# One adding DMA per unit for the sum of the rotated keys, in an attention and feed-forward kernel

## The reference, cut to what matters

```python
def linear_attention(x, Wq, bq, Wk, bk, Wv, bv, g, bb):
    q = gelu(x @ Wq + bq) + 0.21
    k = gelu(x @ Wk + bk) + 0.21
    v = x @ Wv + bv
    q_r, k_r = rope(q), rope(k)          # rope(t) = t * cos + swapped_pairs(t) * sin
    ...                                  # split into 16 heads
    z = 1.0 / (einsum('bhnd,bhmd->bhnm', q, kmean) + 1e-06)
    kv = einsum('bhnd,bhne->bhde', k_r, v) / n
    out = einsum('bhnd,bhde->bhne', q_r, kv) * z
    return layernorm(out + x, g, bb)
```

## Time and profile before

| what | value |
|---|---|
| median of 3 runs | 1835.23 us (1830.85 to 1835.43) |
| the profiled execution | 1831.92 us |
| its span, first to last instruction | 1830.1 us |
| PE busy | 1807.1 us, 99% |
| PEld busy | 1477.9 us, 81% |
| DVE busy | 1454.8 us, 79% |
| POOL busy | 1016.3 us, 56% (over nine tenths within attention) |
| ACT busy | 937.0 us, 51% |
| share of PE in the chain that ended last | 96% |

### The profile page before, as it was taken

How to read it: one execution, slowest core, us unless ns; L and a number is a source line. 1 busy time by engine, 2 the same in 40 slices (tenths; PEclk the granted TensorE clock), 3 DMA queues, 4 the chain that set the end, 5 groups by cost and what they waited for, 6 DMA issues and landing times.

```text
span 1830.1 us, 46210 instructions
## 1 busy us (share of the span) xinstructions
PE 1807.1 (99%) x19196; PEld 1477.9 (81%) x19196; DVE 1454.8 (79%) x3454; ACT 937.0 (51%) x1741; POOL 1016.3 (56%) x775
## 2 busy tenths in 40 slices
PE   9999999999999999999999999999999999999998
PEld 3336888888888888888887988888888888888887
DVE  3667788888788888888887767888888888888887
ACT  5554776677667766677667742232323232323231
POOL 1557999999899999999984012222222222222221
PEclk9999999999999999999999999999999999999999
DMA  8372210100102210000105931010101010101000
GB/s 296 149 270 109 94 60 3 37 2 2 37 2 106 94 37 3 30 9 3 60 2 192 306 105 35 28 42 24 47 24 47 24 47 24 46 25 43 27 12 24
DMA packets 25234, 115.38 MB, mean 63 GB/s; under 512 B 4480, under 2 KB 5440, under 8 KB 19904
## 3 DMA queue, kind: packets, MB, share of 16 engines
q1 hardware_dynamic: 21104, 89.69, 13.9%
q0 software_dynamic: 1152, 12.58, 1.9%
q10 hardware_dynamic: 2768, 10.15, 1.5%
HBM read 80.95 MB, written 31.46 MB: 61 GB/s over the span
## 4 chain that ended last, share of the span: by engine, by line
PE 96%; DVE 2%; issue 1%; DMA 1%; ACT 1%; POOL 0%; ACTq 0%; SPq 0%; DVEq 0%; POOLq 0%
PE bankC L1449 13%; PE bankC L33 7%; PE bankC L32 7%; PE bankC L34 7%; PE ring L32 6%; PE ring L34 6%; PE ring L33 6%; PE bankC L1448 6%; PE big L934 5%; PE big L34 3%; PE big L33 3%; PE big L32 3%; PE ring L866 3%; PE big L846 3%; PE conv_ps L256 3%; PE hid_ps L245 3%
## 5 line engine op out<-in xcount | busy, mean ns | idle before, releaser
L1449 PE MATMUL bankC<-down,act_hi 128*128 128x512 f32 x992 | 353.1, 397 | 0.0
L1448 PE MATMUL bankC<-down,act_lo 128*128 128x256 f32 x868 | 246.2, 284 | 0.0
L1449 PEld LDWEIGHTS bankC<-down,act_hi 128*128 128x128 f32 x992 | 186.3, 188 | 41.9
L1574 DVE TENSOR_TENSOR act_lo<-gel,act_hi 128x512 fp32r<-128x512 f32 x256 | 210.6, 823 | 8.7
L33 PE MATMUL bankC<-aT_lo,up_hi 128*128 128x512 f32 x512 | 199.6, 390 | 0.0
L32 PE MATMUL bankC<-aT_hi,up_hi 128*128 128x512 f32 x512 | 199.5, 390 | 0.0
L34 PE MATMUL bankC<-aT_hi,up_lo 128*128 128x512 f32 x512 | 199.4, 389 | 0.0
L1528 POOL TENSOR_TENSOR hC<-hC,vecC 128x1024 f32<-128x1024 f32 x16 | 38.7, 2416 | 283.5 <-PE turn L1423 283.5
L1534 POOL TENSOR_TENSOR rstdC<-var_epsC,minus_halfC 128x4 f32<-128x4 f32 x47 | 56.1, 1193 | 249.2 <-DVE var_epsC L1602 249.2
L1448 PEld LDWEIGHTS bankC<-down,act_lo 128*128 128x128 f32 x868 | 164.1, 189 | 1.4
L774 POOL TENSOR_TENSOR kr<-kr,kc 128x512 f32<-128x512 f32 x128 | 161.8, 1299 | 0.0
(11 more groups left out here) (215 smaller groups left out, 5261.4 us busy)
## 6 DMA issues: line engine op xcount, KB each, us to landing
raw_late<-in_AB SPq DMA_DIRECT2D x30, 320.0 KB, 3.9
u<-hA SPq DMA_DIRECT2D x8, 1024.0 KB, 5.0
u_next<-u SPq DMA_DIRECT2D x8, 1024.0 KB, 5.9
hC<-u SPq DMA_DIRECT2D x16, 512.0 KB, 3.9
xC<-in_x SPq DMA_DIRECT2D x16, 512.0 KB, 4.8
out<-w_flat SPq DMA_DIRECT2D x15, 512.0 KB, 2.6
w_flat<-in_AB SPq DMA_DIRECT2D x22, 320.0 KB, 3.7
w_split<-w_parts ACTq DMA_DIRECT2D x4, 1536.0 KB, 5.8
```

The lines of the kernel that those rows point to most:

```text
L1448: e.matmul(bank[:, 0:H], a_lo[:, fb, tok], both[k][:, 0, fb, :], start=False, stop=False)
L1449: m = e.matmul(bank[:, :], a_hi[:, fb, tok], both[k][:, :, fb, :], start=fb == 0, stop=fb == FB - 1)
L1574: e.tensor_tensor(a_lo[:, fb, :], g, a_hi[:, fb, :].bitcast(F32), ALU.subtract).then_inc(s_act_lo, 1)
```

## The change

`sum_k` loses its index u. GpSimd waits until all four parts of the unit are rotated, and then issues one DMA with an adding accumulate, which reads `kc` and adds it to `kr` in SBUF. The semaphore s_kr becomes the DMA's semaphore d_kr, which stands at 16 x (n + 1) once unit n has landed. TensorE waits for that value before the first matmul of `key_value(n)`, and the three waits for later parts fall away. VectorE's `rotate_k(n)` waits for unit n - 1 as a whole.

```diff
-            def sum_k(n, u):
-                w.wait_ge(s_ks, 4 * n + u + 1)
-                e.tensor_tensor(kr[:, u, :], kr[:, u, :], kc[:, u, :], ALU.add).then_inc(s_kr, 1)
+            def sum_k(n):
+                w.wait_ge(s_ks, 4 * n + 4)
+                e.dma_start(flat(kr), flat(kc), accum_op=ALU.add).then_inc(d_kr, 16)
...
-                for u in range(DUOS):
-                    sum_k(n, u)
+                sum_k(n)
...
-                        w.wait_ge(s_kr, 4 * n + u + 1)
+                        w.wait_ge(d_kr, 16 * (n + 1))
...
-                w.wait_ge(s_kr, 4 * (n - 1) + u + 1)
+                w.wait_ge(d_kr, 16 * n)
...
-        free = {"hT": [(s_v, 4 * UNITS)], "gkT, kc": [(s_kt, 4 * UNITS), (s_kr, 4 * UNITS)],
+        free = {"hT": [(s_v, 4 * UNITS)], "gkT, kc": [(s_kt, 4 * UNITS), (d_kr, 16 * UNITS)],
```

More of the change, by code:

```diff
@@ L673, in attention_phase @@
         s_memset, s_hT, s_hi, s_lo, s_mul, s_res = (sem(n) for n in ("memset", "hT", "hi", "lo", "mul", "res"))
-        s_k, s_gk, s_kt, s_ks, s_kr = (sem(n) for n in ("k", "gk", "kt", "ks", "kr"))
+        s_k, s_gk, s_kt, s_ks, d_kr = (sem(n) for n in ("k", "gk", "kt", "ks", "d_kr"))
         s_q, s_gelu, s_gq, s_qr, s_qd, s_v, s_vs = (sem(n) for n in ("q", "gelu", "gq", "qr", "qd", "v", "vs"))
```

## The result

The changed kernel takes 1847.9 us (median of 4, 1843.2 to 1850.6); the kernel before, measured again beside it, 1833.6 us. The ratio is 1.0078 (95% interval 1.0066 to 1.0090): slower by 14.3 us, 0.8%. The range held the time, and the chance of slower (0.50) was the largest of the three signs, but the forecast case itself, no change at 1838.1 us, did not come.

A forecast was written before the change was run, and what follows sets the result against it. PE, busy 99% of the span, was taken as the bound. Unit 0's 1.85 us and unit 31's 1.0 us gave 2.85 us on 1831.92, 1834.8; with 3.3 us from profiled run to median, 1838.1 us, range 1831 to 1930.

The forecast's parts named there:

- What bounds the kernel: Whole span: PE is busy 99%, so taking 5.05 us per unit off POOL takes nothing off the end.
- D: The adding DMA's time from issue to landing, bounded between 4.2 and 12.2 us and taken as 7.7 us.
- The choice between the bounds: Adding DMA's landing: two reads set it, 6.7 to 8.7 us, rather than plain-copy cost, 4.2, or three passes, 12.2.
- The estimate of 5.8 us from the Trainium skill: Adding DMA: 259 GB/s on 16 engines, 4.1 us of data plus 1.7 us around it, hidden in every unit.
- Quiet units: Units 3 to 15 and 19 to 30: landing of 7.7 us under a 9.6 us window, cost 0.
- unit 0's lateness: Unit 0's window is only 5.85 us, so the sum comes 1.85 us late for PE.
- unit 31: Last unit: the weights' prefetch adds 2.5 us, so 10.2 against 9.17 us, 1.0 us late (0 to 4).
- The five loaded units: Units 1, 2, 16, 17, 18: a load, or load and store, shares the window; 9.6 against 9.57 us, put at 0.
- what is queued behind that wait: POOL's queue after the fourth part: six rotate_q products, then residual, which PE releases; residual would wait 3.9 us, not 2.90.
- PE's three waits fewer: PE's waits per unit: it waits for none of them now, 7.3 us idle bounds a gain; taken as 0.
- The rival that named the pauses: Dense product L934: fewer waits may shift or remove 9 pauses (5.7 us); 1829.5 us if all went, chance 0.08.
- the second rival: Sum late at L903 only where the window is short or shared, D 8.1 to 9.6 us: 1845 us, chance 0.18.

The follow-up runs named there:

- the plain copy: The changed kernel with a plain copy of kc over kr in place of the adding DMA, the sum left out: 1839.3 us in a single execution.
- the settled GpSimd: The changed kernel; in unit 0 GpSimd writes a small tile after issuing the adding DMA and waits for it before its query products: 1842.8 us, single execution.
- the run with gaps: The changed kernel; in unit 0 alone GpSimd waits for its own finished pair of query products before the next pair: 1843.1 us, 1.0043.

## Why the prediction came out as it did

**What bounds the kernel** was read rightly: taking the sums off POOL gained nothing. With the five disturbed units left out, the DMA kernel is at 0.9997 of before.

**D** was right to 10%: 7.7 us taken, 7.0 us in a unit with nothing beside it and 7.3 in the median. The choice between the bounds, that two reads set it, is supported by the plain copy at 4.7 us. The estimate of 5.8 us from the Trainium skill was under the measured 7.0, though its reason, two source reads ("Collectives: The Full Stack", "The bandwidth ceiling: the fold count and why AG ≠ RS ≠ AR"), agrees with the difference to the copy. In unit 5 the adding DMA's data run from 1.5 to 6.7 us after the issue began, 5.2 us for two reads of 1.05 MB, which is near the 5.0 us of the row at 420 GB/s, and 1.8 us lie around them, near my 1.7. I had taken 6.0 us of data, between the two rates.

**Quiet units** at 0, **unit 0's lateness** at 1.85 us (measured 1.96) and **unit 31** at 1.0 us (1.09) were right in size, with luck in two of them. In unit 0 the 7.7 us came true (7.64) only since a packet of instructions held back the last count by 0.6 us. In the quiet units I counted 1.9 us to spare, but the issue comes 0.3 us after the last rotated part, and beside a packet the sum landed after up to 9.33 us; in unit 27 nothing was left, and it was 0.07 us late.

**The five loaded units** at 0 were wrong: 1.63, 0, 0.96, 1.49 and 0 us, 4.1 in all. The sharing with the load and the store, which I put at 1.9 us in unit 17, was right for 15 of the 16 counts: they had come by 8.85 us, 1.85 us over the 7.0. The step that failed is the list of what runs into the window: it had no term for the packets of PE's instructions. In unit 17 one was in flight beside the data, and the last count came at 10.76 us, 1.9 us after the others. It is alike in units 1 and 16: 15 counts by 9.33 and 9.22 us, at the edge of the 9.3 us that PE leaves, and the last at 10.90 and 10.22 us. In unit 18, with the load and the store but no such packet, all had come by 8.44 us. In units 16 and 17 it takes both causes to make the sum late by 1 us and more, as far as these traces show; why a packet of 16 KB holds back one count by up to 2.3 us is open.

**Unit 0 beyond the lateness** had no term: 5 us. The step that failed is "what is queued behind that wait", which I asked of POOL's own queue only. POOL's products now start 4.3 us sooner and right behind a DMA issue, and I never asked which VectorE instruction stands beside them. The plain copy, with no late sum, lost 7.4 us here, and the settled GpSimd, with a late sum and nothing held, 2.5 us. The trace of before gave a hint in the same place: this instruction took 0.48 us there at its longest, against 0.17 in the median. The Trainium skill states in "SBUF — State Buffer", "Who interferes with whom", that VectorE and GpSimd share a pair of ports, that `tensor_scalar` can be an instruction that needs it, and that the other then blocks fully. This case agrees and goes beyond it: in the runs right behind a DMA issue the block lasted not for one GpSimd instruction, but for six.

**PE's three waits fewer** at 0 were wrong in both directions: 2.6 us gained in L902, 6.9 us lost in longer and more frequent pauses. The rival that named the pauses priced them at -5.7 us and said that they might as well only move; they moved to where they cost more. The run with one wait and no DMA has 3.8 us of the 6.9, and the others with that count differ among themselves (9.4 to 13.6 us of pauses), so one trace of each kernel does not tell how much of the 6.9 us the change brings every time. The lengths go for the most part with how late a packet ends; what makes it late is not shown.

So the second rival, late in few units only (1845 us, chance 0.18), is the nearest to what came: its sign, five to seven waits of the keys' product for a DMA, came true with five. But it had the sum for other reasons than its own: D was in the forecast's own range, and 5 of its 9.9 us stood for all five loaded units, where three were late. That its 1845 us lie 3 us from the measured 1847.9 is in part luck. It has no term for VectorE in unit 0 either.

## What to carry to other kernels

Work taken off an engine that is not the bound gains nothing, but what replaces it can cost at the few places where its window is short or shared: list these one by one, and count among what runs beside a transfer the packets that bring an engine's instructions, which here held back the last count of the semaphore and not the bulk of the data. When instructions of GpSimd move in time, look at VectorE's short instructions beside them too, above all where a run of GpSimd follows the issue of a DMA without a pause. In a kernel that PE bounds at 99%, the pauses that wait for "issue" are the gain that is left: here placing the dense product within the instruction packets, with waits hidden under large matmuls, was worth 9 us.

## What the runs showed of the hardware

- An adding DMA of 1 MB within SBUF lands 7.0 us after GpSimd begins to issue it where nothing runs beside it, a plain copy of the same bytes 4.7 us after in the median, an adding one of 512 KB 4.9 us after in the median. Its issue takes 0.92 us, a plain one 0.64 us.
- Beside a load of 1 MB, or a load and a store, the adding DMA of 1 MB lands after 8.4 to 10.9 us (units 1, 2, 16, 17 and 18 of the kernel after).
- Beside packets of instructions alone (16 KB, in most units one) it lands after 7.4 to 9.3 us. In units 8 and 21, 15 of its 16 counts had come by 7.0 us, and the last came at 9.2 us.
- A VectorE `tensor_scalar` of 128 x 4 was held for 7.43 to 8.60 us by GpSimd's run of products right behind a DMA issue, and for 0.48 us (the kernel before) and 0.57 us (the settled GpSimd) by runs with no DMA issue right ahead of them, to the end of one GpSimd instruction.
- PE pauses of 0.6 to 2.0 us in a product of short matmuls follow the place of the product within packets of 256 instructions. Their length goes for the most part with how late the packet's transfer ends. In the longest pause of the kernel after, PE's chain reads:

```profile
351.55 1.92 PE big L933 x72
353.47 1.40 issue
354.87 1.36 PE big L933 x47
```

- PE's granted clock fell to 0.50 at 187.0 us of the kernel after, behind idle stretches of 1.77, 0.48 and 2.60 us, and at 181.5 us of the run with gaps, behind one of 1.77 us and at the start of one of 0.52 us. In the run with the settled GpSimd it stayed at 1.00 behind 1.76 and 0.51 us, so these stretches alone do not decide it.
